# A gated cross-attention and quantised-FFN block on one core: five hand-written engine orders exchanged for five others

## The reference

```python
# x (16, 224, 512), context (16, 750, 384), mask (16, 750); 8 heads of 64
xn   = layernorm(x)
q, k, v = xn @ W_q, ctx @ W_k, ctx @ W_v
sim  = where(mask, q k^T / 8, -max)
x    = x + tanh(g_xattn) * (softmax(sim) v @ W_o + b_o)
xn   = layernorm(x)
h    = bitlinear(xn, w1, b1)          # 512 -> 2048
h    = gelu(h)
x    = x + tanh(g_ffn) * bitlinear(h, w2, b2)     # 2048 -> 512
```

## Time and profile before

| | us |
|---|---|
| median of 3 executions | 1109.84 |
| lowest and highest | 1105.44, 1114.69 |
| the profiled execution, its own time | 1107.53 |
| its span in the profile | 1105.3 |
| TensorE busy in the span | 1017.3 |

### The profile page before, as it was taken

The page is one execution under the profiler, slowest core; times in us unless marked ns, Lnnn a source line. Parts: engine busy times, 40 slices in busy tenths (PEclk is TensorE's granted clock), DMA queues, the critical chain, the costliest instruction groups (busy, mean ns, idle before and its releaser), DMA issues.

```text
span 1105.3 us, 24267 instructions
## 1 busy us (share of the span) xinstructions
PE 1017.3 (92%) x8576; PEld 601.6 (54%) x8576; DVE 821.2 (74%) x1774; ACT 845.0 (76%) x1458; POOL 768.2 (69%) x743
## 2 busy tenths in 40 slices
...
GB/s 226 200 177 226 193 141 156 150 175 147 110 194 122 167 134 159 160 134 188 148 144 127 162 173 134 164 148 152 126 166 152 162 151 138 142 125 127 164 106 39
DMA packets 472135, 168.83 MB, mean 153 GB/s; under 512 B 450384, under 2 KB 452176, under 8 KB 471632
## 3 DMA queue, kind: packets, MB, share of 16 engines
...
## 4 chain that ended last, share of the span: by engine, by line
PE 28%; POOL 19%; ACT 14%; DMA 14%; issue 11%; DVE 10%; SPq 3%; ACTq 0%; DVEq 0%; POOLq 0%
PE ps_g L733 14%; POOL p L1285 9%; DMA pt<-p 7%; PE ps_s L763 4%; PE ps_g L790 3%; PE ps_g L829 3%; DMA hqt<-hq 3%; PE ps_g L866 3%; SPq L697 2%; ACT prob L1128 2%; DMA xqt<-xq 2%; POOL p L1280 2%; ACT hq L1244 2%; POOL ctx L1296 2%; DVE prob L948 1%
## 5 line engine op out<-in xcount | busy, mean ns | idle before, releaser
L1285 POOL TENSOR_TENSOR p<-prob,p 112x750 f16<-112x750 f32 x256 | 408.6, 1608 | 78.7 <-ACT p L1135 77.0
L948 DVE CUSTOM_DVE_ANT_0 prob<-ps_s,mbias 112x750 f32<-112x750 f32 x256 | 236.8, 935 | 81.4 <-PE ps_s L763 53.6
L1128 ACT ACTIVATE prob<-prob,rmin 112x750 f32<-112x750 f32 x256 | 233.3, 913 | 32.4 <-DVE rmin L948 32.0
L733 PE MATMUL ps_g<-ctx,wk 128*128 128x375 f16 x1152 | 199.2, 325 | 17.4 <-DVE wk L901 16.1
L733 PE MATMUL ps_g<-wv,ctx 128*128 128x512 f16 (+1 forms) x864 | 197.1, 380 | 3.1 <-DVE k_sb L972 1.9
L763 PE MATMUL ps_s<-k_sb,q_sb 64*112 64x375 f16 x1536 | 151.1, 330 | 19.9 <-DVE rmin L948 19.0
L733 PEld LDWEIGHTS ps_g<-ctx,wk 128*128 128x128 f16 x1152 | 109.5, 98 | 97.3 <-issue 25.1
L1135 ACT ACTIVATE p<-prob 112x750 f16<-112x750 f32 x160 | 129.5, 820 | 20.0 <-DMA pt<-p 19.8
L733 PEld LDWEIGHTS ps_g<-wv,ctx 128*128 128x128 f16 (+1 forms) x864 | 86.7, 103 | 97.9 <-issue 4.1
L1280 POOL CAST p<-prob 112x750 f16<-112x750 f32 x96 | 77.9, 812 | 83.2 <-DMA pt<-p 48.4
L763 PEld LDWEIGHTS ps_s<-k_sb,q_sb 64*112 64x112 f16 x1536 | 90.9, 127 | 74.8 <-issue 38.6
...
## 6 DMA issues: line engine op xcount, KB each, us to landing
...
pt<-p SPq DMA_TRANSPOSE x256, 4.0
...
```

The source lines that it names most:

```text
L733: mm = nc.tensor.matmul(out, lhs, rhs, start=(m == 0), stop=(m == len(steps) - 1))
L948: nc.vector.tensor_tensor_reduce(prob[:, (b * NU + n) % PROBS, :].rearrange("p (c k) -> p c k", c=2), ps_s[0:HT, n % 2, :, 0:CH], mbias[:, ...
L1128: nc.scalar.activation(prob[:, (b * NU + n) % PROBS, :], prob[:, (b * NU + n) % PROBS, :], ACT.Exp, bias=rmin[:, n:n + 1], scale=-1.0, acc ...
L1285: nc.gpsimd.tensor_tensor(p16[:, u % HILO, 1, 0:J], prob[:, (b * NU + n) % PROBS, :], p16[:, u % HILO, 0, 0:J], ALU.subtract).then_inc(s[" ...
```

## The change

All five lists are replaced by others. Each new list holds exactly the items of the old one (496 on SyncE, 670 on TensorE, 1071 on ScalarE, 993 on VectorE, 628 on GpSimd, counted from the lists). The new lists are made with more room for late landings of the turnings. No buffer, no instruction, no wait is changed. The start of four of the lists, and the stretch of TensorE's in which the last two batches end:

```diff
 SP_SEQ
-    PD:0:0 LX:0:0 LC:0:0 LC:2:0 LC:1:0 PD:1:0 WL:0:0 XT:0:0 LM:0:0 PD:2:0 XT:1:0 LX:0:1 WL:1:0 LC:1:1 LC:0:1 LM:0:1
+    PD:0:0 LC:0:0 LX:0:0 LC:1:0 LC:2:0 PD:1:0 WL:2:0 PD:2:0 XT:1:0 XT:0:0 WL:1:0 WL:0:0 LM:0:0 LX:0:1 WL:3:0 WL:4:0
...
 PE_SEQ
-    K:0:0 K:1:0 K:2:0 K:3:0 K:4:0 K:5:0 K:6:0 Q:0:0 S:0:0 V:0:0 V:1:0 S:1:0 V:2:0 V:3:0 V:4:0 V:5:0 Q:1:0 Q:2:0
-    K:7:0 S:2:0 S:3:0 S:4:0 Q:3:0 WM:0:0 PV:0:0 S:5:0 V:0:1 V:1:1 V:2:1 K:0:1 S:6:0 K:1:1 V:3:1 Q:0:1 K:2:1 K:3:1
+    K:0:0 K:1:0 K:2:0 K:3:0 K:4:0 Q:0:0 Q:1:0 Q:2:0 S:0:0 V:0:0 K:5:0 V:1:0 S:1:0 V:2:0 V:3:0 V:4:0 V:5:0 K:6:0
+    K:7:0 S:2:0 S:3:0 Q:3:0 S:4:0 WM:0:0 K:0:1 V:0:1 S:5:0 PV:0:0 V:1:1 V:2:1 V:3:1 S:6:0 K:1:1 K:2:1 Q:0:1 S:7:0
...
-    PV:3:14 V:4:15 V:5:15 S:4:15 O:0:14 O:1:14 PV:0:15 PV:1:15 F2:1:13 F1:0:14 F1:1:14 F1:2:14 F1:3:14 TX:1:14
-    S:5:15 S:6:15 PV:2:15 F1:4:14 S:7:15 PV:3:15 F1:5:14 PV:4:15 F1:6:14 F1:7:14 O:0:15 PV:5:15 F2:0:14 PV:6:15
+    PV:3:14 V:4:15 S:4:15 V:5:15 O:0:14 O:1:14 PV:0:15 PV:1:15 F2:1:13 F1:0:14 F1:1:14 F1:2:14 F1:3:14 TX:1:14
+    S:5:15 PV:2:15 F1:4:14 S:6:15 S:7:15 F1:5:14 PV:3:15 F1:6:14 F1:7:14 PV:4:15 PV:5:15 O:0:15 F2:0:14 PV:6:15
...
 ACT_SEQ
-    CX:0:0 PW:0:0 CX:1:0 CX:2:0 XH:0:0 K:0:0 XH:1:0 K:1:0 K:2:0 K:3:0 K:4:0 PW:1:0 PW:2:0 WA:0:0 K:5:0 K:6:0
+    PW:0:0 CX:0:0 CX:1:0 CX:2:0 XH:0:0 XH:1:0 PW:1:0 K:0:0 K:1:0 K:2:0 PW:2:0 K:3:0 K:4:0 Q:0:0 Q:1:0 WA:0:0
...
 DVE_SEQ
-    N1:0:0 XN:0:0 PW:0:0 XH:0:0 KL:0:0 XH:1:0 KL:1:0 KL:2:0 KL:3:0 KL:4:0 PW:1:0 PW:2:0 QL:0:0 M:0:0 M:1:0
+    PW:0:0 N1:0:0 XN:0:0 XH:0:0 XH:1:0 PW:1:0 KL:0:0 KL:1:0 KL:2:0 KL:3:0 QL:0:0 KL:4:0 PW:2:0 M:0:0 M:1:0
...
 POOL_SEQ
-    N1:0:0 CX:0:0 CX:1:0 CX:2:0 MB:0:0 L:0:0 L:1:0 H:2:0 N1:0:1 L:2:0 CX:0:1 L:3:0
+    CX:0:0 N1:0:0 CX:1:0 CX:2:0 MB:0:0 N1:0:1 L:0:0 L:1:0 H:2:0 L:2:0 L:3:0 CX:0:1
```

More of the change, by code:

```diff
@@ new lines @@
+    T:8:3 HT:0:2 T:9:3 LC:1:5 T:10:3 T:11:3 LC:0:5 T:12:3 HT:1:2 LR:1:3 T:13:3 T:14:3 T:15:3 T:0:4 LC:2:5 XT:1:5
+    XT:0:5 T:1:4 LX:0:6 F2:0:2 T:2:4 XQ:0:3 T:3:4 LC:0:6 XQ:1:3 T:4:4 T:6:4 T:7:4 T:5:4 LR:1:4 LM:0:5 T:8:4 HT:0:3
+    LC:1:6 T:9:4 T:10:4 LX:0:7 T:11:4 T:12:4 LM:0:6 T:13:4 HT:1:3 T:14:4 T:15:4 XT:1:6 XT:0:6 T:0:5 F2:0:3 LC:2:6
+    T:1:5 T:3:5 F2:1:2 T:2:5 LC:1:7 T:4:5 LC:0:7 T:5:5 T:6:5 XQ:1:4 T:7:5 T:8:5 T:9:5 LR:1:5 T:11:5 T:10:5 LR:0:5
+    T:12:5 T:13:5 HT:1:4 T:15:5 T:14:5 LC:2:7 T:0:6 F2:1:3 F2:1:4 XT:1:7 XT:0:7 T:2:6 T:1:6 T:3:6 XQ:0:5 T:4:6
@@ new lines @@
+    LR:1:6 T:5:6 LX:0:8 LM:0:7 T:7:6 T:6:6 T:8:6 XQ:1:5 LR:0:6 T:9:6 HT:0:5 LC:0:8 T:10:6 T:11:6 T:12:6 LC:1:8
+    T:13:6 HT:1:5 T:14:6 T:15:6 LC:2:8 F2:0:5 T:0:7 T:1:7 XT:1:8 XT:0:8 T:2:7 LX:0:9 XQ:0:6 T:3:7 T:4:7 LM:0:8
+    LR:0:7 T:5:7 T:6:7 T:7:7 XQ:1:6 F2:1:5 T:8:7 HT:0:6 LC:0:9 T:9:7 T:10:7 T:11:7 T:12:7 T:13:7 HT:1:6 LC:1:9
+    T:14:7 T:15:7 LR:1:7 LX:0:10 T:0:8 LC:2:9 XT:1:9 XT:0:9 F2:0:6 T:1:8 XQ:0:7 T:2:8 LC:0:10 T:4:8 T:3:8 T:5:8
+    T:7:8 LM:0:9 T:6:8 XQ:1:7 T:8:8 T:9:8 HT:0:7 T:11:8 F2:1:6 T:10:8 LR:1:8 T:12:8 T:13:8 LC:1:10 HT:1:7 T:14:8
@@ new lines @@
+    T:6:11 T:5:11 T:7:11 T:8:11 XQ:1:10 HT:0:10 T:9:11 T:10:11 T:11:11 T:12:11 LC:1:13 T:13:11 HT:1:10 T:14:11
+    T:15:11 LX:0:14 T:0:12 LC:2:13 T:1:12 XT:1:13 F2:1:10 XT:0:13 T:3:12 T:2:12 XQ:0:11 LC:0:14 T:4:12 F2:0:10
+    T:5:12 LR:1:12 T:6:12 T:7:12 T:8:12 LM:0:13 XQ:1:11 HT:0:11 LR:0:13 T:9:12 T:10:12 T:11:12 LC:1:14 T:12:12
+    T:13:12 HT:1:11 T:15:12 T:14:12 T:0:13 LC:2:14 T:1:13 LX:0:15 T:2:13 F2:1:11 T:3:13 F2:0:11 T:4:13 XT:0:14
+    XT:1:14 T:5:13 T:7:13 T:6:13 LR:1:13 T:8:13 LM:0:14 XQ:1:12 T:9:13 T:10:13 T:11:13 LC:1:15 LC:0:15 T:12:13
@@ new lines @@
+    K:4:5 PV:1:4 S:7:4 F1:4:3 F1:5:3 F1:6:3 F1:7:3 K:5:5 F2:0:3 V:4:5 V:5:5 Q:2:5 S:0:5 PV:2:4 S:1:5 K:6:5 K:7:5
+    Q:3:5 F2:1:3 S:2:5 PV:3:4 S:3:5 Q:0:6 O:1:4 S:4:5 Q:1:6 V:0:6 V:1:6 S:5:5 PV:0:5 K:0:6 K:1:6 V:2:6 V:3:6 S:6:5
+    K:2:6 K:3:6 F1:4:4 F1:5:4 F1:6:4 F1:7:4 S:7:5 PV:1:5 K:4:6 K:5:6 V:4:6 V:5:6 S:0:6 PV:2:5 S:1:6 Q:2:6 K:6:6
+    K:7:6 S:2:6 F2:1:4 PV:3:5 S:3:6 Q:3:6 O:0:5 O:1:5 K:0:7 Q:0:7 S:4:6 Q:1:7 V:0:7 V:1:7 F1:0:5 F1:1:5 F1:2:5
+    F1:3:5 PV:0:6 S:5:6 V:2:7 V:3:7 K:1:7 K:2:7 K:3:7 K:4:7 S:6:6 PV:1:6 S:7:6 F1:4:5 F1:5:5 F1:6:5 F1:7:5 K:5:7
@@ L153 @@
+    F3:1:15
 """)
 ACT_SEQ = in_order("""
[L155 to L158 removed]
@@ L219 @@
[L219 to L221 removed]
+    PW:0:0 CX:0:0 CX:1:0 CX:2:0 XH:0:0 XH:1:0 PW:1:0 K:0:0 K:1:0 K:2:0 PW:2:0 K:3:0 K:4:0 Q:0:0 Q:1:0 WA:0:0 WA:1:0
+    WA:2:0 Q:2:0 E:0:0 E:1:0 V:0:0 K:5:0 V:1:0 H:0:0 XH:0:1 H:1:0 XH:1:1 V:2:0 V:3:0 WA:3:0 E:2:0 E:3:0 V:4:0 WA:4:0
@@ new lines @@
+    H:3:0 WA:5:0 CX:0:1 WA:6:0 CX:1:1 E:4:0 WA:7:0 K:6:0 H:4:0 Q:3:0 V:5:0 CX:2:1 K:7:0 E:5:0 E:6:0 PW:3:0 E:7:0
+    K:0:1 E:8:0 V:0:1 H:6:0 PV:0:0 E:9:0 H:8:0 WG:0:0 V:1:1 V:2:1 V:3:1 H:9:0 E:10:0 E:11:0 K:1:1 E:12:0 PL:0:0
+    H:11:0 K:2:1 WA:8:0 XH:0:2 XH:1:2 H:12:0 Q:0:1 E:13:0 PV:1:0 E:14:0 Q:1:1 WA:9:0 PL:1:0 K:3:1 K:4:1 K:5:1
+    WA:10:0 H:14:0 WA:11:0 E:15:0 E:0:1 E:1:1 PV:2:0 K:6:1 H:0:1 K:7:1 E:2:1 V:4:1 H:1:1 E:3:1 CX:0:2 V:5:1 Q:2:1
+    H:3:1 PL:2:0 WA:12:0 E:4:1 PV:3:0 WA:13:0 CX:1:2 PL:3:0 Q:3:1 WA:14:0 CX:2:2 WA:15:0 E:5:1 H:4:1 E:6:1 E:7:1
@@ new lines @@
+    H:6:5 Q:1:6 E:8:5 V:0:6 V:1:6 E:9:5 L4:1:4 H:8:5 PV:0:5 K:0:6 PL:0:5 K:1:6 E:10:5 H:9:5 V:2:6 V:3:6 E:11:5
+    E:12:5 E:13:5 K:2:6 K:3:6 H:11:5 H:12:5 GE:1:4 E:14:5 PV:1:5 GS:1:4 PL:1:5 K:4:6 E:15:5 K:5:6 V:4:6 H:14:5
+    G3:1:4 PV:2:5 V:5:6 E:0:6 Q:2:6 E:1:6 H:0:6 H:1:6 E:2:6 CX:0:7 K:6:6 CX:1:7 XH:0:7 XH:1:7 K:7:6 PL:2:5 E:3:6
+    PV:3:5 PL:3:5 H:3:6 E:4:6 H:4:6 CX:2:7 E:5:6 E:6:6 Q:3:6 L4:0:5 E:7:6 Q:0:7 K:0:7 Q:1:7 H:6:6 V:0:7 V:1:7 E:8:6
+    E:9:6 GE:0:5 PV:0:6 GS:0:5 V:2:7 H:8:6 K:1:7 V:3:7 H:9:6 K:2:7 L4:1:5 E:10:6 E:11:6 K:3:7 K:4:7 G3:0:5 PV:1:6
@@ new lines @@
+    PL:0:10 E:10:10 V:3:11 K:3:11 K:4:11 E:11:10 G3:0:9 PV:1:10 H:11:10 E:12:10 H:12:10 XH:0:12 K:5:11 E:13:10
+    PL:1:10 GE:1:9 V:4:11 GS:1:9 E:14:10 G3:1:9 V:5:11 H:14:10 Q:2:11 E:15:10 E:0:11 PV:2:10 XH:1:12 K:6:11 H:0:11
+    CX:0:12 PL:2:10 E:1:11 CX:1:12 H:1:11 K:7:11 E:2:11 PV:3:10 PL:3:10 E:3:11 E:4:11 H:3:11 H:4:11 E:5:11 CX:2:12
+    E:6:11 Q:3:11 Q:0:12 E:7:11 Q:1:12 L4:0:10 E:8:11 K:0:12 V:0:12 H:6:11 V:1:12 E:9:11 GE:0:10 H:8:11 K:1:12
+    GS:0:10 V:2:12 PV:0:11 E:10:11 V:3:12 L4:1:10 PL:0:11 K:2:12 K:3:12 E:11:11 K:4:12 H:9:11 G3:0:10 PV:1:11
@@ new lines @@
+    G3:1:13 V:5:15 E:6:15 E:7:15 E:8:15 E:9:15 PV:0:15 L4:0:14 PL:0:15 PV:1:15 H:6:15 H:8:15 H:9:15 L4:1:14 PL:1:15
+    TX:1:14 GE:0:14 PV:2:15 E:10:15 E:11:15 GS:0:14 H:11:15 E:12:15 E:13:15 G3:0:14 PL:2:15 H:12:15 PV:3:15 E:14:15
+    PL:3:15 E:15:15 H:14:15 PV:4:15 GE:1:14 PL:4:15 PV:5:15 GS:1:14 PL:5:15 PV:6:15 PL:6:15 PV:7:15 PL:7:15 G3:1:14
+    L4:0:15 TI:2:14 TX:0:15 TI:3:14 L4:1:15 TX:1:15 GE:0:15 GS:0:15 ZE:0:15 ZE:1:15 ZS:0:15 ZE:2:15 G3:0:15 ZS:1:15
+    ZS:2:15 ZE:3:15 ZS:3:15 TI:0:15 TI:1:15 Z3:0:15 Z3:1:15 Z3:2:15 TI:2:15 Z3:3:15 TI:3:15
@@ new lines @@
+    VL:5:13 PA:2:12 KL:6:13 M:4:13 M:5:13 XH:0:14 XH:1:14 F2:1:11 KL:7:13 PA:3:12 M:6:13 QL:2:13 QL:3:13 O:1:12
+    M:7:13 L2:1:12 KL:0:14 M:8:13 M:9:13 VL:0:14 PA:0:13 KL:1:14 M:10:13 KL:2:14 VL:1:14 M:11:13 N1:0:15 KL:3:14
+    L3:1:12 QL:0:14 XN:0:15 QL:1:14 VL:2:14 M:12:13 VL:3:14 M:13:13 PA:1:13 F1:4:12 KL:4:14 F1:5:12 F1:6:12 F1:7:12
+    M:14:13 M:15:13 GM:1:12 G2:1:12 M:0:14 M:1:14 KL:5:14 VL:4:14 VL:5:14 M:2:14 M:3:14 KL:6:14 PA:2:13 M:4:14
+    F2:1:12 M:5:14 KL:7:14 QL:2:14 PA:3:13 XH:0:15 M:6:14 XH:1:15 O:0:13 M:7:14 QL:3:14 L2:0:13 O:1:13 L3:0:13
@@ new lines @@
+    M:8:14 M:9:14 L2:1:13 VL:0:15 VL:1:15 PA:0:14 KL:0:15 M:10:14 M:11:14 F1:0:13 F1:1:13 F1:2:13 KL:1:15 L3:1:13
+    QL:0:15 F1:3:13 M:12:14 M:13:14 KL:2:15 KL:3:15 KL:4:15 M:14:14 GM:0:13 M:15:14 QL:1:15 PA:1:14 VL:2:15 G2:0:13
+    VL:3:15 F1:4:13 M:0:15 F1:5:13 F1:6:13 F1:7:13 M:1:15 KL:5:15 M:2:15 M:3:15 KL:6:15 KL:7:15 QL:2:15 M:4:15
+    M:5:15 PA:2:14 QL:3:15 GM:1:13 M:6:15 M:7:15 F2:0:13 G2:1:13 PA:3:14 VL:4:15 M:8:15 VL:5:15 M:9:15 O:0:14
+    L2:0:14 L3:0:14 PA:0:15 O:1:14 L2:1:14 PA:1:15 L3:1:14 F2:1:13 F1:0:14 F1:1:14 F1:2:14 F1:3:14 M:10:15 M:11:15
```

432 lines of the change are left out of this document (191 added, 241 removed).

## The result

| | us |
|---|---|
| before, median of the paired executions (lowest to highest) | 1109.22 (1105.44 to 1114.69) |
| after, median of 4 | 1065.36 (1062.81 to 1068.74) |
| after : before, 95% interval | 0.9603 (0.9552 to 0.9654) |
| the profiled execution of after, and its span | 1063.77, 1061.8 |

The forecast was 1101, with 1088 as its lower end. Where two experiments are compared, the ratios are the fairer measure; the new kernel's own ratio is known to 5.6 us either way.

A forecast was written before the change was run, and what follows sets the result against it. The prediction took TensorE, busy 1017.3 of 1105.3 us, as the bound, with only its 88 idle us open to change. Its terms, 7 + 1.6 + 0.3 = 8.9 us less, gave 1101 us, range 1088 to 1114.

The forecast's parts named there:

- First K at 14.6: Start: with W_k's split first on ScalarE and VectorE, TensorE starts at 14.6 us, 1.4 us earlier.
- S:0 at 26.8, S:3 and S:4 with 3.3 us: Start: first scores near 26.8 instead of 31.79; S:3 and S:4 wait 3.3 us in all, 3.7 less.
- GpSimd can follow by 7.1: Up to the first F1: GpSimd's last FFN weight scaling moves 7.1 us earlier; 7 us taken, bounds 2 and 15.
- Of the 6.0 us I take half, 3: Middle, 150 to 1000 us: half of TensorE's turning waits go, FFN landing waits stay; 1.6 less after new S costs.
- the sign of being wrong: Middle: the prediction is wrong if TensorE's idle time there moves by more than 8 us either way.
- The change can act on its 88 idle us only: Whole kernel: no order changes TensorE's work, so only its 88 idle us of 1105.3 can change.
- The clock: Start, 53.2 to 63.4 us: TensorE's granted clock is 0.50; nothing for it was taken in the sum.
- the rival's 2.6: Start opens wider: TensorE keeps its clock, 2.6 us come back, 14.2 less in all, 1095.6; chance 0.27.
- Seven more one-PV places, 1.4 us: Middle: S follows S with only one PV between in 23 places, not 16; costs 1.4 us.
- bare scores: Middle: 23 places with too little cover wait up to 1.0 us each, costing 23, giving 1125.5; chance 0.10.
- GpSimd has 31% slack, so most of that costs nothing: Whole kernel: turnings hold up GpSimd for 48.4 us, but most of that costs nothing because of its slack.
- The end, 0.3: Last batch: S:6 waited 2.45 us, now S:7 waits 2.2 behind it; 0.3 us less, bounds 3 either way.

The follow-up runs named there:

- o_pad: Kernel before, with one more 4-byte DMA issued by SyncE behind each turning (transpose of probabilities): 1131.70 us against 1110.62, ratio 1.0175.
- n_pad: Kernel after, with one more 4-byte DMA issued by SyncE behind each turning: 1068.37 us, ratio 0.9605 to the kernel before.
- o_ring5: Kernel before, with p16 holding five units instead of four, so H waits for the turning five units back: 1105.24 us against 1109.58, ratio 0.9966.
- x_head: New lists up to the first F1, the old order behind it: 1101.24 us against 1112.61 for the kernel before, ratio 0.9905.
- x_rest: Old lists up to the first F1, the new order behind it: 1079.15 us, ratio 0.9705 to the kernel before.
- o_half: Kernel before, turning only the high half of the probabilities from the seventh unit on: 1081.82 us, ratio 0.9734.
- n_half: Kernel after, turning only the high half of the probabilities from the seventh unit on: 1061.94 us, ratio 0.9555 to the kernel before.
- x_head_half: New lists up to the first F1, old order behind it, only the high half of the probabilities turned: 1074.91 us, ratio 0.9695 to the kernel before.

## Why the prediction was wrong, step by step

- **First K at 14.6**: it came at 14.67, behind GpSimd's last subtraction, as worked out.
- **S:0 at 26.8, S:3 and S:4 with 3.3 us**: 27.8 and 2.5. Right within 1 us. The late 1.0 is in the first K items: 16 matmuls start 0.31 us apart there before the pace is 0.16, where the kernel before had 10 (counted from the traces; the granted clock is given as 1.00).
- **"GpSimd can follow by 7.1", 7 us for the first 150**: wrong in size, 12.1. Up to the first F1 GpSimd's idle time fell by 15.3 us (49.1 to 33.8, the windows from 0 to 149.88 and to 137.84) while its busy time grew by 3.3. I had moved its first L and left its other waits, some 30 us, as they were. Its last scaling came 17 us earlier. The range that I gave the term, 2 to 15, held this.
- **"Of the 6.0 us I take half, 3. The waits for the FFN's landings stay, as the least work between O and F1 is 9.5 us in both lists"**: the step that failed, with its outer bound of 9 us less. Measured, the middle's idle time fell by 24.0 us, three times the 8 us that I had named as the sign of being wrong. In all the middle gained 27.6 us for the same items (30.6 between the two cuts), 1.6 forecast. I priced the change with the one wait whose name it carried and took the other waits for a floor. The view had a third row of landings, 5.4 us for HT, that I left out altogether.
- **What the runs showed in its place**: room at many places under many names. The room between O and F1 was a minimum over the lists, and it is equal; but tiles with at most 10 us of it are 6 before and 3 after, and from the issue of XQ to its F1 there were 5.6 us in the mean before and 6.7 after, at least 2.6 and 3.1 (counted from the traces). The landing alone takes 2.9 in the median and 5.5 at most. The like for HT: 5.9 and 7.8 us in the mean, and its landing takes 4.8. For turnings, 50 of 192 units had under 5.5 us from the issue of the transpose to the H that reuses its place before, 30 after. On TensorE, where I saw no room gained by the mean of the work ahead of a PV, 14 of 49 PVs of the middle started within 0.5 us of their last landing before and 6 of 52 after, while the mean from the last issue to the PV hardly moved (7.1 and 7.3 us). The count of GpSimd work that I did make (6.9 to 8.2 us) pointed the right way. A chain that is just in time at many places shows up under the names of whatever is last there: a drain, a row minimum, another transfer of the queue. The landings of all transposes went from 18.2 us to 1.8, and `o_pad` and `n_pad` show it by experiment: the same small delay costs 21 us and 3 at most.
- **"The change can act on its 88 idle us only"**: not quite. TensorE's busy time fell by 6.3 us (1017.3 to 1011.0), 3.6 of it in the middle. There the clock doesn't explain it: the kernel before has no stretch at 0.50 in its middle, the new one has one of 3.4 us, from 668.2 on. The busy time of a matmul has a modelled end, so I can't tell shorter matmuls from matmuls recorded with less of a wait in them.
- **The clock**: left out of the sum, and the stretch at 0.50 shrank from 10.2 to 6.8 us with 6.10 of it busy. At the upper level 3.05 of these would go, so the rival's 2.6 did not come back. A second stretch in the start before, 3.4 us from 118.1 on, is absent after.
- **Seven more one-PV places, 1.4 us; rival "bare scores"**: no such cost. In the middle cut by work the row minimum's waits are 4.2 us, 3.1 before, with 23 places of that kind in place of 16, but these places themselves cost 0.8 in both (counted from the traces).
- **"GpSimd has 31% slack, so most of that costs nothing"**: its 48.4 us of waits for turnings did not cost by their length, and `o_ring5` confirms that (4 us). They were the sign of the late chain all the same.
- **The end, 0.3**: 0.8 by the cuts, 3.8 for the same items. S:6 and S:7 of the last batch, the only waits in the sum, went from 2.5 and 1.0 us to 0.4 and 2.5, which is 0.6 less, twice the forecast; the rest had no term.

Shown by the runs: the start is worth 10 to 12 us and the order behind it some 32, independent of each other (`x_head`, `x_rest`); the old order pays for queue time where the new one hardly does (`o_pad`, `n_pad`); the old order gains from shorter turnings where the new one hardly does (`o_half`, `n_half`). Argued from rows alone: that the some 10 us between `x_head_half` and the new kernel are the PSUM bank of line 1095, the row minimum and HT. Open: how much of the cut's gain is the shorter flight and how much the lighter load on the DMA engines; what makes up the 6.3 us of busy time; and which of the five lists does it, since no run exchanged one of them alone.
